# Routed experts: a place of its own for each of 39 tiles of rows and results

## The reference

```python
x = x + graph_attention(layernorm(x), adj)      # cosine scores, softmax over neighbours
x = x + routed_ffn_0(layernorm(x)[None])        # one routing decision for all rows
x = x + graph_gather(layernorm(x), adj)         # att = exp(e[j]-max) over neighbours, att @ inp
x = x + routed_ffn_1(layernorm(x)[None])        # two of eight experts for each row
```

## Time and profile before

| what | value |
|---|---|
| median of the runs | 834.89 us (834.57, 834.89, 837.68) |
| span of the profiled execution | 873.3 us |
| PE busy | 723.2 us (83%) |
| DVE busy | 571.8 us (65%) |
| ACT busy | 491.2 us (56%) |
| POOL busy | 196.0 us (22%) |
| routed stage, first row load to the end of the last result scatter | 693.1 to 850.1 us |
| read back, add, store | 850.1 us to the end |

### The profile page before, as it was taken

The page is one execution under the profiler, slowest core; times in us unless marked ns, Lnnn a source line. Parts: engine busy times, 40 slices in busy tenths (PEclk is TensorE's granted clock), DMA queues, the critical chain, the costliest instruction groups (busy, mean ns, idle before and its releaser), DMA issues. The chain is left out here.

```text
span 873.3 us, 11391 instructions
## 1 busy us (share of the span) xinstructions
PE 723.2 (83%) x3372; PEld 424.4 (49%) x3372; DVE 571.8 (65%) x1658; ACT 491.2 (56%) x741; POOL 196.0 (22%) x233
## 2 busy tenths in 40 slices
PE   2758999999999999999929978799899785776740
PEld 1543444444444444444418966354445374665640
DVE  7785668788888878787864787556555662534325
ACT  1746888888888888888827785222312241222210
POOL 2240000000000000000005531015434456565560
PEclk9969999999999999999958997799999876889875
DMA  4108989899999989887530000401100122222208
GB/s 130 69 0 262 288 260 262 255 273 253 259 258 260 272 249 275 243 255 223 165 128 8 1 2 0 122 5 39 33 25 29 56 67 68 73 79 74 79 18 288
DMA packets 100893, 124.58 MB, mean 143 GB/s; under 512 B 9038, under 2 KB 78930, under 8 KB 100576
## 3 DMA queue, kind: packets, MB, share of 16 engines
q1 hardware_dynamic: 96288, 115.32, 45.9%
q0 software_dynamic: 4544, 8.54, 3.0%
HBM read 88.54 MB, written 36.20 MB: 143 GB/s over the span
## 5 line engine op out<-in xcount | busy, mean ns | idle before, releaser
L552 DVE SCALAR_TENSOR_TENSOR probs<-adj,probs 128x1024 f32<-128x1024 int32 x128 | 156.7, 1224 | 77.0 <-ACT probs L525 68.0
L475 PE MATMUL ps<-x,qT 128*128 128x512 f16 x768 | 188.0, 382 | 3.2 <-PEq L198 3.2
L525 ACT ACTIVATE probs<-ps 128x1024 f32<-128x1024 f32 x128 | 130.9, 1023 | 51.0 <-PE ps L475 51.0
L536 ACT ACTIVATE mask<-probs 128x1024 fp8e4<-128x1024 f32 x128 | 134.0, 1047 | 0.0
L487 PE MATMUL ps<-probs,v 128*128 128x512 f32 x256 | 130.8, 592 | 0.0
L1397 PE MATMUL ps<-mask,parts 128*128 128x512 fp8e4 x512 | 119.7, 391 | 8.1 <-DVE parts L1664 8.1
L475 PEld LDWEIGHTS ps<-x,qT 128*128 128x128 f16 x768 | 75.5, 98 | 94.7 <-issue 5.7
L1571 ACT ACTIVATE mask<-ps,mask 128x256 f32<-128x256 f32 x78 | 32.6, 471 | 101.3 <-PE ps L1482 46.7
L1647 POOL DMA_INDIRECT mixed_spill<-mask,xn x78 | 76.3, 978 | 57.0 <-DVE mask L1794 32.3
L558 DVE TENSOR_TENSOR p_lo<-probs,p_hi 128x512 f16<-128x512 f32 x128 | 87.6, 684 | 0.1
L1600 POOL DMA_INDIRECT sorted_rows_spill<-rows,slots x64 | 62.8, 982 | 99.5 <-issue 54.4
(11 more groups left out here) (289 smaller groups left out, 975.3 us busy)
## 6 DMA issues: line engine op xcount, KB each, us to landing
adj<-in_adj SPq DMA_DIRECT2D x128, 512.0 KB, 4.8
sorted_rows_spill<-blank SPq DMA_DIRECT2D x32, 528.0 KB, 6.7
sorted_rows_spill<-blank SPq DMA_DIRECT2D x26, 198.0 KB, 7.4
xn<-sorted_rows_spill SPq DMA_DIRECT2D x39, 132.0 KB
mask<-mixed_spill SPq DMA_DIRECT2D x8, 512.0 KB, 6.3
mask<-in_x SPq DMA_DIRECT2D x4, 512.0 KB, 5.8
feat_spill<-mask SPq DMA_DIRECT2D x8, 256.0 KB
x_feat<-in_x SPq DMA_DIRECT2D x8, 256.0 KB, 4.8
```

What stands on the lines that cost most here:

```text
L475: ins = nc.tensor.matmul(out, qT[:, q_half, j], kT[:, c, k_half * GROUP:(k_half + 1) * GROUP], start=(n == 0), stop=(n == 2))
L525: nc.scalar.activation(probs[:, k % RING, :], ps[:, b:b + 2, :].rearrange("p b n -> p (b n)"), ACT.Exp, scale=1.0 / QK_SCALE ** 2).then_in ...
L536: nc.scalar.activation(mask[:, k * W:(k + 1) * W], probs[:, k % RING, :], ACT.Sign, saturate=False).then_inc(mask_kept, 1)
L552: nc.vector.scalar_tensor_tensor(out=probs[:, k % RING, :], in0=adj[:, k % LOADS, :], scalar=0.0, in1=probs[:, k % RING, :], op0=ALU.is_gt ...
```

## The change

Rows and results get 39 places each (`ROUTED_STEPS`) in place of eight, both in the room of the mask; an assertion keeps them out of the mask's last eighth, which the last chunk still reads. The room of `xn` isn't used any more. The scatters count on one semaphore, `y_out`, in place of eight. VectorE's wait for the scatters of tile k - 8 goes. SyncE's wait before load k is now for the landing of load k - 8, so at most eight loads are under way. The final wait is one wait for all 78 scatters.

```diff
--- before.py
+++ after.py
@@ -1292,16 +1292,16 @@
         rest_table, moved_on = sem("rest_table"), sem("moved_on")
 
         room = Carver(sb["mask"][:, :].bitcast(F32))
-        xn_room = Carver(sb["xn"][:, :, :].rearrange("p t d -> p (t d)"))
         RING = 4
         LOADS = 8
         WEIGHTS = 3
         current = room.take(WEIGHTS, EXPERT_WIDTH)
         tokens = room.take(RING, 2 * P)
         hT = room.take(SLOTS, FH, 2 * P)
-        y = room.take(LOADS, 2, D)
+        y = room.take(ROUTED_STEPS, 2, D)
         both = room.take(RING, 2, SUB, D)
-        sorted_rows = xn_room.take(LOADS, 2, ROW)
+        sorted_rows = room.take(ROUTED_STEPS, 2, ROW)
+        assert room.used <= (GROUPS - 1) * TILES * GROUP // 4
@@ -1313,7 +1313,7 @@
-        y_out = [sem(f"y_out{u}") for u in range(LOADS)]
+        y_out = sem("y_out")
@@ -1360,11 +1360,10 @@
                     start = sp.value_load(table[0:1, 1, k:k + 1], min_val=0, max_val=E * N + (ROUTED_STEPS - 1) * 2 * P)
                     if k >= LOADS:
 
-                        sp.wait_ge(y_out[u], 32 * (k // LOADS))
-                    sp.dma_start(sorted_rows[:, u, :, :], io["sorted"][bass.ds(start, 2 * P), :].rearrange("(h p) n -> p h n", p=P))\
+                        sp.wait_ge(rows_in[u], 16 * (k // LOADS))
+                    sp.dma_start(sorted_rows[:, k, :, :], io["sorted"][bass.ds(start, 2 * P), :].rearrange("(h p) n -> p h n", p=P))\
                         .then_inc(rows_in[u], 16)
-                for u in range(LOADS):
-                    sp.wait_ge(y_out[u], 32 * len(range(u, ROUTED_STEPS, LOADS)))
+                sp.wait_ge(y_out, 32 * ROUTED_STEPS)
@@ -1469,7 +1468,7 @@
-                        ins = nc.tensor.transpose(ps[:, XT_BANK + k % 2, h * P:(h + 1) * P], sorted_rows[:, u, h, 0:D], sb["ident"][:, :])
+                        ins = nc.tensor.transpose(ps[:, XT_BANK + k % 2, h * P:(h + 1) * P], sorted_rows[:, k, h, 0:D], sb["ident"][:, :])
@@ -1646,8 +1644,8 @@
                     for h in range(2):
                         nc.gpsimd.indirect_dma_start(
                             out=io["mixed"][:, :],
-                            out_offset=bass.IndirectOffsetOnAxis(ap=sorted_rows[:, u, h, D:D + 1].bitcast(U32), axis=0),
-                            in_=y[:, u, h, :], in_offset=None, bounds_check=2 * N - 1, oob_is_err=False).then_inc(y_out[u], 16)
+                            out_offset=bass.IndirectOffsetOnAxis(ap=sorted_rows[:, k, h, D:D + 1].bitcast(U32), axis=0),
+                            in_=y[:, k, h, :], in_offset=None, bounds_check=2 * N - 1, oob_is_err=False).then_inc(y_out, 16)
@@ -1787,11 +1785,8 @@
                     dve.wait_ge(down_ready, k + 1)
-                    if k >= LOADS:
-
-                        dve.wait_ge(y_out[k % LOADS], 32 * (k // LOADS))
                     bias = current[:, k % WEIGHTS, 2 * F:2 * F + D].unsqueeze(1).to_broadcast([P, 2, D])
-                    nc.vector.tensor_tensor(y[:, k % LOADS, :, :], ps[:, Y_BANK + k % 2, 0:2 * D].rearrange("p (h d) -> p h d", d=D), bias, ALU.add)\
+                    nc.vector.tensor_tensor(y[:, k, :, :], ps[:, Y_BANK + k % 2, 0:2 * D].rearrange("p (h d) -> p h d", d=D), bias, ALU.add)\
                         .then_inc(y_ready, 1)
```

More of the change, by code:

```diff
@@ L1638, in _ @@
                 for k in range(ROUTED_STEPS):
-                    u = k % LOADS
                     if k == SCATTER_AT:
```

## The result

The changed kernel takes 844.67 us (four runs, 843.94 to 846.67) against 834.74 us before: a ratio of 1.011, interval 1.009 to 1.013. It is slower, by 7.5 to 9.9 us; 833.0 was forecast, and the time lies outside the range.

A forecast was written before the change was run, and what follows sets the result against it. GpSimd's scatter queue was taken to pace the routed stage's end. From 834.89 us, 1.7 for the loads and 0.1 for the final wait were subtracted, giving 833.1, said as 833.0 us; range 826.5 to 839.

The forecast's parts named there:

- part 4 of the change: SyncE after the last scatter: eight final waits become one, -0.3 us at most, taken as -0.1 us.
- Rival C: Slower: 22 loads in one burst share DMA engines with GpSimd's scatters, which wait for descriptor room; 7.1 us, 842; chance 0.11.
- Rival D: Slower: VectorE's 39 weight copies hold back GpSimd's descriptor writing, 182 ns a scatter, 7.1 us, to 842; chance 0.03.
- late waits: Late starts in the profiled routed stage, perhaps largely absent when timed; GpSimd's starving plus expert choice's remote waits, 36.8 us.
- nothing waits behind SyncE: Routed stage: SyncE waits 43.1 us for landed scatters before loads, but nobody is seen waiting behind it.
- Item 3: SyncE's loads wait for load k-8 instead of scatters: gain 1.7 us without late waits, bounds 0 and 5.4 us.
- The stop at turn 10: TensorE at the tenth row turn stands 3.7 us for load 10, held by tile 2's scatters, then restarts slowly.
- bias add 8: VectorE's eighth bias add, put at 738.0 in the kernel before; GpSimd free for tile 8 only at 742.5.
- bias add 10: VectorE's tenth bias add, put about 4 us after the ninth, at 747.8, leaving GpSimd starved for 1.7 us.
- VectorE's removed wait: Wait for y_out before 31 of 39 bias adds, always met when reached: gain taken as 0, bound 0.9 us.
- Rival B: Faster: without the ring of eight the chain runs ahead over late waits; 823 to 830.5 us, middle 829; chance 0.26.
- Rival E: SyncE's new wait could pace the burst so slowly that loads come no earlier: no effect; inside A's 0.60.

The follow-up runs named there:

- the second trace of before: The kernel before, unchanged, run and traced again: 835.57 us, ratio 1.000, span 835.4 us.
- the run with the loaded rows in their ring: The kernel before with 39 places for results alone and without VectorE's wait; loaded rows in eight places in xn's room, loads paced by scatters: 835.44 us, ratio 0.999.
- the three other kernels with unpaced loads and no interruption: The changed kernel with two semaphores in turn (835.86 us), a new one each six tiles (836.41), or six of 78 scatters on another (836.47).

## Why the prediction was wrong

**The step that failed is part 4 of the change**, the only one that puts a price on the move from eight semaphores to one. I priced the single `y_out` only at its final wait, -0.1 us on SyncE, and never asked what the 78 increments onto it do on the engine that issues the scatters, although GpSimd's queue was the thing that I had found to end the stage. That cost stood at nothing; it measured +8.6 us in five interruptions. The final wait itself was sized well: SyncE's first read starts 2.23 us behind the start of the last scatter in the second trace of before (811.72 to 813.95) and 2.09 us in the changed kernel (819.16 to 821.25). No rival named the shared semaphore either: C put a shortage of room for descriptors down to the burst of loads. That C and D both priced a slower kernel at 842 us, near the measured time, is luck; neither cause was at work.

**What bounds the kernel: right.** GpSimd's queue paces the stage; 73 steps of 1.28 us from tile 2's first scatter are 93 us, and before takes 94.3. The argument that the 38.4 us between the profiled and the timed execution are its late waits is borne out: in the second trace they are gone and the span is 835.4; from tile 2's first scatter to the last it is 27.6 us shorter than the earlier trace rows, and that first scatter comes 9.8 us sooner. Why the first had them stays open. The sentence that nothing waits behind SyncE was a fact of that trace alone; in the other one TensorE waits 35.7 us for loads.

**Item 3, the loads: right in kind, 1.7 us too much.** The stop at turn 10 is there (6.57 us idle, 3.7 forecast), and bias add 9 comes 5.77 us behind bias add 8 (5.8). Two terms were mis-sized. Bias add 8 was 732.76 - 727.61 = 5.2 us ahead of its scatter's turn, not 742.5 - 738.0 = 4.5. And bias add 10 came 2.2 us behind bias add 9, where I had taken 3.95 from the earlier trace rows, a pair with 2.57 us of idle time between them against 0.81 in the second trace, in a working that was to have no late waits. So bias add 9 still started 2.2 us ahead of its scatter (733.38 to 735.58), where 1.2 us are needed, later ones no less, and GpSimd never ran short: the gain is 0. In the changed kernel bias add 8 is at 718.12 and the last turn 20.3 us sooner (777.1 against 797.4), and none of it reaches the end.

**VectorE's removed wait: right, 0** (the run with the loaded rows in their ring: 0.999).

**Rival B**, that the lead covers late waits, has nothing to cover in an undisturbed run. **Rival C** is refuted by its own sign: the 22 loads leave behind the table and are all issued by 748.8, and the scatters' median stays 972 ns. What the burst may cost is the 1.8 us between the runs with unpaced and with paced loads and eight semaphores, at most; the three other kernels with unpaced loads and no interruption lie at 1.0005 to 1.0008. **Rival D**, the port, is refuted too: the longest scatter of after is 1137 ns, the mean 982 against 978. **Rival E** is refuted by SyncE's waits of after.

A version that beats both kernels doesn't follow from these runs: without the interruptions all variants end within 0.2% of before, since GpSimd needs its 94 to 95 us in each.

## What to carry to other kernels

Ask of each change what it does to the queue that ends the stage, its semaphore increments included: let the DMAs that GpSimd issues back to back count on two or more semaphores in turn, or at least change over before the descriptor scratch is full. A deeper ring for an engine that has work in hand ahead of the bound bought nothing here. And compare the span of a trace with the timed median before reading waits out of it: 38 us between them meant that the waits in it weren't those of the timed runs.

## What the runs showed of the hardware

- With 2048 bytes a partition of descriptor scratch, 14 indirect scatters of 128 rows in a row on one semaphore are followed by a pause of GpSimd of 1.8 to 2.7 us in place of 0.30; with 1024 bytes the pause comes after seven (1.7 to 2.5 us). With 12 in a row, or with one increment in twelve on another semaphore, it doesn't come. I read the 14 and the seven as what the scratch holds.
- The Trainium skill (DMA: Bandwidth & Descriptors, section "Terms") gives a descriptor 16 bytes, and for a 1 MiB transfer to 128 partitions it counts 9 descriptors per engine and side (section "The descriptor swizzle"). If a scatter of 128 rows takes as many, and one partition of the scratch holds those of one engine and side, an estimate from these figures is 2048 / 16 / 9 = 14.2 scatters, and 7.1 with half the scratch. The rows agree with both, 14 and 7.
- The length of the pause fits a wait for the newest scatter's landing: in the changed kernel the next starts 2.75 to 3.66 us behind the start of the last one, the longest of these falls in the burst of loads, and the very last scatter has landed 2.1 us behind its start, when SyncE's first read goes out. The oldest of the 14 started 17 us before the newest, so it has long landed by then. That room is given back only up to the last scatter of a run on one semaphore is my reading of it; the runs show when the pause comes, not what GpSimd does in it.
- The Trainium skill (the same page, DMA: Bandwidth & Descriptors, section "Why a DMA increments its semaphore by 16 and not by 1") asks for one semaphore per slot in flight, so that counts can't be mistaken. No run here shows a mistaken count, as the changed kernel waits only for all of them; what they show is that sharing one also cost time.
